# Chunk 6's ranks moved into the first batch, and eight shared chunks dealt 3, 2, 3 instead of 2, 1, 5

## The chip, the cores and the metric

One core of a Trainium2 chip runs the kernel. The metric is device time in microseconds (us) of one execution, lower is better. Before the change it is 659.68 us, the median of three runs (657.02 to 660.19).

## The reference

A state-space and convolution block with a dense MLP, then a mixture of experts, each followed by a layer norm. Batch 4 x 1024 tokens, width 128, float32. Cut to what matters:

```python
# first block
y = rmsnorm(x) * norm_w
x = x + conv3(y) + scan(tanh(a), b * y)          # along the 1024 tokens
x = x + down(silu(gate(rmsnorm(x))) * up(rmsnorm(x)))   # hidden 512
x = layernorm(x0 + x)
# second block: 64 experts of width 88 in 8 groups; 2 shared experts (176)
scores = sigmoid(x @ gate_w.T)
c = scores + gate_bias
group_scores = sum of the two largest c of each group   # keep the 4 best groups
masked = where(group kept, c, 0)
topk = the 8 largest of masked                   # experts of a token
w = 2.5 * scores[topk] / sum(scores[topk])
out = sum_k w_k * expert_k(x) + shared(x)        # expert: silu(x Wg) * (x Wu) Wd
x = layernorm(x + out)
```

## The kernel before

The 4096 tokens are 32 tiles of 128, in eight chunks of four tiles (512 tokens). Chunks 0 to 6 (28 tiles) are routed, that is, each token is sent to its eight experts. Chunk 7 is not: it goes through all 64 experts densely, with weights that are zero for experts not chosen. The routed tiles form two batches of 14 tiles.

**Front.** A loop over nine steps (`step` on TensorE, the loop over `k` on the other engines) does the first block, one chunk per step, with the routing of earlier chunks between: scores (ScalarE, `scores`), group sums and masks (VectorE, `group_sums`, `group_seconds`, `compare_groups`, `mask_groups`), the choice of eight (`choose`), and the rank of each token within its expert (`ranks`, a stream of bf16 matmuls against 0/1 tables; `take_ranks`). A rank gives the slot, a row of a DRAM buffer with a region of 2048 rows per expert. After the last chunk of a batch its table is made: `count_tiles`, `starts`, `place_tiles`, `tile_experts`, `weight_columns`. It says for each of the batch's 176 tiles of 128 slots which expert's weights and which rows belong to it.

**Scatters.** GpSimd copies every tile's tokens to their slots, eight indirect DMAs a tile, 224 in all (line 513), in order of tiles. It waits once per chunk for that chunk's slots.

**Prelude.** After the front come the two first shared chunks (`shared_block`: two blocks of two matmuls into the bank GU; a SiLU on ScalarE; `shared_hidden`, a product on VectorE; `shared_down` into the bank XT or OT; `add_shared`). Among them stand the last chunk's norm, transposition and logits, chunk 6's ranks and the second batch's table. ScalarE does root and norm of chunk 7 before the first SiLU. At the end VectorE makes all gather slots of the first batch (`gather_slots`).

**Batches.** A batch is 44 quads of four expert tiles. SyncE loads a quad's rows (line 444), from the moment that all scatters of that batch have landed. TensorE does for quad q: `tr_x` (q + 2), `gate_up` (q + 1), `tr_h` (q, line 829), `down` (q - 1). ScalarE copies x (line 1077), does the SiLU (1084), copies the output (1094) and stores it. VectorE does `mul_h` (q + 1, line 1513) and `take_h` (q, line 1522), and after it whatever stands at that quad: `slot_weights` (three operations of 512 elements; one tile at each odd quad from quad 1), the steps of chunk 7's choice (quads 2, 4, 6, 8, 10), two `gather_slots` of the second batch (12, 14), from quad 60 `add_round`. Each engine works strictly in its own written order, so an operation set between two quads holds back the next quad's. `tr_h` of the next quad needs the bank HT, hence `take_h` of this one.

One shared chunk stands between the batches, five after the second.

**Gathers and additions.** GpSimd fetches each token's eight results back by indirect DMAs (line 518), in eight sets of up to four tiles through two buffers; VectorE adds them with their weights (`add_round`, line 1576). The sets 0 to 3 belong to the first batch, 4 to 7 to the second. Ahead of the first set of a batch GpSimd waits for all stores of that batch:

```python
if ts[0] == TFIRST[b]:
    pool.wait_ge(s_gslot, 2 * b + 1)
    for r in range(4):
        pool.wait_ge(d_st[r], 4 * Q0[b + 1])
```

**Dense part.** After the last shared chunk TensorE runs 44 steps (lines 880, 881, 889) for chunk 7. Between them VectorE adds the sets 4 to 7 (`SUMS_IN_DENSE`: set: first step, rounds per step, rounds at most) and takes the statistics of the finished chunks (`STATS_IN_DENSE`, `ROOT_AT`). The last rounds, the last statistics, the norm and the last output follow.

Of the kernel before, what the change touches and what calls it, by code (L numbers as in the profile page):

```python
# [37 lines left out]
P = 128  # L38
# [9 lines left out]
E = 64  # L48
# [28 lines left out]
WT = 2  # L77
KT = 8
SH_A, SH_B = 2, 3
# [37 lines left out]
SUMS_IN_DENSE = {4: (2, 2, 8), 5: (10, 1, 8), 6: (26, 1, 8), 7: (38, 1, 5)}  # L117
STATS_IN_DENSE = {0: 0, 1: 1, 2: 2, 7: 3, 19: 4, 35: 5}
ROOT_AT = (5, 21, 37)
# [20 lines left out]
def build(nc, x, vecs, w_gate, w_up, w_down, b_down, gate_wT, gate_bias, wgu, wd, wdf, sgu, sd, out, xs, os):  # L140
    with ExitStack() as ctx:
# [25 lines left out]
        eps = sb("eps", [P, 2])  # L167
        ident = sb("ident", [P, P])
# [59 lines left out]
        score = cut(CT, E)  # L228
# [136 lines left out]
        def keys_in_psum():  # L365

            return MI[:, :].rearrange("p (t e) -> p t e", e=E)

# [109 lines left out]
        def _(pool):  # L478
# [43 lines left out]
            for g_, ts in enumerate(SETS):  # L522
# [3 lines left out]
                if ts[0] == TFIRST[b]:  # L526
                    pool.wait_ge(s_gslot, 2 * b + 1)
                    for r in range(4):
                        pool.wait_ge(d_st[r], 4 * Q0[b + 1])
# [13 lines left out]
        def _(pe):  # L543
# [102 lines left out]
            def ranks(c):  # L646
# [6 lines left out]
                mm(HT[:, 0:CT * E], ones_bf[:, :], base_bf[:, :].unsqueeze(1).to_broadcast([P, CT, E]),  # L653
                   start=True, stop=False, skip_group_check=True)
                for b in range(NBAT):
                    own = [t for t in tiles(c) if batch_of(t) == b]
                    for s in range(TFIRST[b], own[-1] if own else 0):
                        lo = max(s + 1, own[0]) - c * CT
                        n = own[-1] - c * CT + 1 - lo
                        mm(HT[:, lo * E:(lo + n) * E], ones_bf[:, :],  # L660
                           sel[:, s % (4 * CT), :].unsqueeze(1).to_broadcast([P, n, E]), start=False, stop=False,
                           skip_group_check=True)
                ins = mm(HT[:, 0:CT * E], upto_bf[:, :], flat(sel[:, ring(c), :]), start=False, stop=True,
                         skip_group_check=True)
                if c in CLAST:
                    b = CLAST.index(c)
                    for t in range(TFIRST[b], TFIRST[b + 1]):
                        ins = mm(HT[0:E, H_CNT:H_CNT + 1], sel[:, t % (4 * CT), :], ones_bf[:, 0:1],
# [3 lines left out]
            def starts(b):  # L672

                pe.wait_ge(s_nt, b + 1)
                mm(HT[:, H_START:H_START + E], ntile_bf[:, :].to_broadcast([E, P]), upto_bf[0:E, 0:E], start=True,
                   stop=True)
                mm(HT[:, H_NUM:H_NUM + E], count[:, :].to_broadcast([E, P]), ident[0:E, 0:E], start=True,
                   stop=True)
                mm(HT[0:E, H_END:H_END + 1], upto_bf[0:E, 0:E], ntile_bf[:, :], start=True,
                   stop=True).then_inc(p_start, 1)  # L680

            def tile_experts(b):

                pe.wait_ge(s_ended, b + 1)
                mm(HT[0:1, 0:ET[b]], base_col[:, 1:2], onehot[:, 0:ET[b]], start=True, stop=True)
                mm(HT[0:1, H_OFF:H_OFF + ET[b]], row_col[:, 0:1], onehot[:, 0:ET[b]], start=True,
# [68 lines left out]
            def shared_down(c):  # L755
                pe.wait_ge(s_sh, SJ * (c + 1))
                if c == 0:
                    pe.wait_ge(s_x1T, NC)
                elif c == 1:
                    pe.wait_ge(s_v, NC)  # L760
                else:
# [5 lines left out]
                dst = OT if c % 2 else XT  # L767
# [6 lines left out]
            def shared_from(lo, hi):  # L774
                for c in range(lo, hi):
                    shared_block(c, 0)
                    shared_block(c, 1)
                    if c == 0:
                        transpose_x1(NS, NC + 1)
                    if c == 1:  # L780
                        ranks(NS - 1)
                    if c > lo:
                        shared_down(c - 1)
                    if c == 1:
# [979 lines left out]
```

## Time and profile before

| | |
|---|---|
| median of three runs | 659.68 us |
| profiled execution | 659.67 us |
| its span | 657.9 us |
| TensorE matmul (PE), busy | 588.1 us, 89% |
| VectorE (DVE) | 461.0 us, 70% |
| GpSimd (POOL) | 444.8 us, 68% |
| ScalarE (ACT) | 325.7 us, 50% |

The span is the stretch from the first to the last instruction that the profile holds. PEld is TensorE's weight load, which overlaps PE. PEclk is the clock granted to TensorE as a share of full speed (1.0 is 2.4 GHz, 0.5 is 1.2 GHz). In a timeline the first two numbers are start and duration in us, then engine, line of the kernel, operation, output and inputs, how many were merged, and in brackets how long the engine had been idle and what released it ("issue" is nothing that the profile shows). In groups of instructions the columns are line, engine, operation, output and inputs, count, then busy us and mean ns of one, then the idle time ahead of them and what ended most of it.

### The profile page before, as it was taken

How to read it: one execution, taken by the hardware profiler on the slowest of the kernel's cores; microseconds unless marked ns; L12 is line 12 of the kernel's file. 1: busy time of each engine (PE TensorE's matmuls, PEld its weight loads, DVE VectorE, ACT ScalarE, POOL GpSimd, SP SyncE). 2: the span in 40 equal slices, each digit the busy share in tenths (PEclk: the TensorE clock that was granted, in tenths of full speed). 3: DMA queues.
4: the chain of work that ended last, by engine and by line, in shares of the span. 5: the costliest groups of instructions: out<-in, count | busy, mean ns of one | idle time of the engine just before them, and what ended most of it. 6: DMA issues, size and time to landing. Idle time of an engine off the chain costs nothing.

```text
span 657.9 us, 13016 instructions
## 1 busy us (share of the span) xinstructions
PE 588.1 (89%) x3456; PEld 472.5 (72%) x3457; DVE 461.0 (70%) x1311; ACT 325.7 (50%) x637; POOL 444.8 (68%) x464
## 2 busy tenths in 40 slices
PE   2986988888889899999996999999999999999980
PEld 2655666665655899999994999999995666666640
DVE  3446688888756789767773567677475598868785
ACT  8474866665553454555552455555552135252332
POOL 1003777777777777777776777777764777777773
PEclk9988899998997999999998999999999999999995
DMA  8962666661112678777755688888866223222122
GB/s 211 383 133 52 138 156 144 148 141 53 53 49 84 179 230 237 230 227 224 230 159 141 184 235 228 242 232 234 228 198 203 53 53 95 56 69 65 52 65 64
DMA packets 124609, 101.35 MB, mean 154 GB/s; under 512 B 15334, under 2 KB 114494, under 8 KB 124094
## 3 DMA queue, kind: packets, MB, share of 16 engines
q1 hardware_dynamic: 63766, 48.41, 27.9%
q0 software_dynamic: 14336, 29.39, 15.3%
q10 hardware_dynamic: 46464, 23.07, 12.1%
q8 instruction: 16, 0.26, 0.2%
q14 instruction: 27, 0.22, 0.1%
HBM read 52.58 MB, written 48.23 MB: 153 GB/s over the span
## 4 chain that ended last, share of the span: by engine, by line
PE 41%; POOL 31%; issue 12%; DVE 5%; DMA 4%; ACT 3%; SPq 1%; POOLq 0%; DVEq 0%; ACTq 0%
POOL xs_dram L513 29%; PE GU L820 8%; PE OT L840 6%; PE GU L880 4%; PE GU L881 4%; PE XT L889 4%; PE HT L829 3%; PE XT L809 3%; DMA arena<-os_dram,gslots 2%; POOL arena L518 2%; PE GU L601 1%; PE GU L752 1%; PE GU L751 1%; DMA xs_dram<-x1r,slots 1%; SPq L444 1%
## 5 line engine op out<-in xcount | busy, mean ns | idle before, releaser
L513 POOL DMA_INDIRECT xs_dram<-x1r,slots x224 | 225.7, 1007 | 123.5 <-issue 67.5
L518 POOL DMA_INDIRECT arena<-os_dram,gslots x224 | 217.0, 969 | 80.6 <-issue 64.8
L820 PE MATMUL GU<-wgu_sb,arena 128*128 x704 | 121.5, 316 | 0.1
L820 PEld LDWEIGHTS GU<-wgu_sb,arena 128*128 128x128 f32 x704 | 106.3, 192 | 1.2 <-issue 0.9
L1513 DVE TENSOR_TENSOR mlpw_sb<-GU,mlpw_sb 128x352 f32<-128x352 f32 x88 | 46.1, 524 | 73.6 <-ACT mlpw_sb L1084 70.0
L840 PE MATMUL OT<-wd_sb,arena 88*128 x704 | 93.7, 276 | 1.8 <-ACT ol L1094 1.7
L1094 ACT ACTIVATE ol<-OT 128x512 f32<-128x512 f32 x88 | 52.5, 597 | 80.7 <-PE OT L840 80.7
L840 PEld LDWEIGHTS OT<-wd_sb,arena 88*128 88x128 f32 x704 | 85.5, 192 | 3.0 <-issue 2.6
L1576 DVE SCALAR_TENSOR_TENSOR x_all<-arena,wk,x_all 128x128 f32<-128x128 f32 x224 | 66.3, 344 | 4.7 <-DMA arena<-os_dram,gslots 2.8
L1084 ACT ACTIVATE mlpw_sb<-GU 128x352 f32<-128x352 f32 x88 | 40.7, 463 | 49.3 <-PE GU L820 48.7
L1188 ACT ACTIVATE key<-GU 128x512 f32<-128x512 f32 x44 | 26.2, 596 | 69.9 <-PE GU L881 69.8
L1522 DVE COPY arena<-HT 88x512 f32<-88x512 f32 x88 | 59.6, 677 | 0.8 <-PE HT L829 0.8
L809 PE MATMUL XT<-ident,arena 128*128 128x128 f32 x352 | 54.4, 277 | 4.7 <-DMA arena<-xs_dram 3.0
L1077 ACT ACTIVATE arena<-XT 128x512 f32<-128x512 f32 x88 | 52.2, 593 | 12.4 <-PE XT L809 10.2
L829 PE MATMUL HT<-ident,mlpw_sb 128*88 128x128 f32 x352 | 52.8, 273 | 1.6 <-DVE arena L1522 1.6
L880 PE MATMUL GU<-x_all,wgu_sb 128*128 128x512 f32 x88 | 45.8, 602 | 1.5 <-DVE x1r L1487 0.9
L809 PEld LDWEIGHTS XT<-ident,arena 128*128 128x128 f32 x352 | 41.8, 143 | 6.9 <-DMA arena<-xs_dram 4.9
L881 PE MATMUL GU<-x_all,wgu_sb 128*128 128x512 f32 x88 | 44.9, 592 | 0.0
L829 PEld LDWEIGHTS HT<-ident,mlpw_sb 128*88 128x88 f32 x352 | 40.6, 122 | 4.2 <-DVE mlpw_sb L1513 1.3
L601 PE MATMUL GU<-arena,mlpw_sb 128*128 128x512 f32 x64 | 37.5, 671 | 6.8 <-DVE arena L1262 6.0
L1614 DVE TENSOR_TENSOR key<-GU,key 128x512 f32<-128x512 f32 x44 | 30.1, 685 | 18.6 <-PE XT L889 10.3
L880 PEld LDWEIGHTS GU<-x_all,wgu_sb 128*128 128x128 f32 x88 | 28.1, 327 | 17.4 <-issue 8.7
(206 smaller groups left out, 897.2 us busy)
## 6 DMA issues: line engine op xcount, KB each, us to landing
arena<-xs_dram SPq DMA_DIRECT2D x352, 64.0 KB
os_dram<-ol ACTq DMA_DIRECT2D x88, 256.0 KB
xs_dram<-ol SPq DMA_DIRECT2D x16, 512.0 KB
wgu_sb<-wgu_dram SPq DMA_DIRECT2D x1, 5632.0 KB
xs_dram<-x1r,slots POOLq DMA_INDIRECT x224
arena<-os_dram,gslots POOLq DMA_INDIRECT x224, 2.6
wd_sb<-wd_dram SPq DMA_DIRECT2D x1, 2816.0 KB
x_all<-x_dram SPq DMA_DIRECT2D x8, 256.0 KB, 5.7
```

The source lines that it names most:

```text
L513: g.indirect_dma_start(out=xs[b], out_offset=bass.IndirectOffsetOnAxis(ap=slots[:, t * K + k:t * K + k + 1], axis=0), in_=x1r[:, t, :], in ...
L518: return g.indirect_dma_start(out=gbuf[:, g_ % 2, t - SETS[g_][0], k, :], out_offset=None, in_=os[batch_of(t)], in_offset=bass.IndirectOff ...
L809: ins = tr(XT[:, i * P:(i + 1) * P], xl[:, u % 4, i * P:(i + 1) * P], ident[:, :])
L820: ins = mm(GU[:, 2 * r + i // 2, (i % 2) * 2 * I:(i % 2 + 1) * 2 * I], xg[:, r, i * P:(i + 1) * P], wgu_sb[:, bass.ds(at[i], 2 * I)], star ...
L829: ins = tr(HT[0:I, i * P:(i + 1) * P], eh[:, u % 2, i * I:(i + 1) * I], ident[:, :])
L840: ins = mm(OT[:, i * P:(i + 1) * P], hT[0:I, u % 2, i * P:(i + 1) * P], wd_sb[:, bass.ds(at[i], P)], start=True, stop=True)
L880: mm(GU[:, r, :], wgu_sb[:, j:E * 2 * I:I], x1T(NS), start=True, stop=True)
L881: mm(GU[:, r + 1, :], wgu_sb[:, HI + j:E * 2 * I:I], x1T(NS), start=True, stop=True).then_inc(p_dg, 1)
L1077: f(xg[:, u % 2, :], XT[:, :], ACT.Copy).then_inc(s_xg, 1)
L1094: f(ol[:, u % 4, :], OT[:, :], ACT.Copy).then_inc(s_eo, 1)
L1522: v.tensor_copy(hT[0:I, u % 2, :], HT[0:I, :]).then_inc(s_ht, 1)
L1576: v.scalar_tensor_tensor(out=x_all[:, t, :], in0=gbuf[:, g % 2, t - SETS[g][0], kk, :], scalar=wk[:, t * K + kk:t * K + kk + 1], in1=x_all ...
```

## The change

`SH_A` and `SH_B` go from 2, 3 to 3, 5: three shared chunks ahead of the first batch, two between the batches, three after the second. In the prelude the SiLUs of chunks 0 and 1 come ahead of the root and norm of chunk 7; chunk 2's down goes to the bank HT. Chunk 6's `ranks` follow quad 1 of the first batch on TensorE, `starts` quad 3, `tile_experts` quad 5, now in the bank MI; VectorE has the steps that belong to them, and the first batch's gather slots in two halves, among quads 1 to 6. Chunk 7's choice moves to quads 5, 7, 8, 10 and 13, slot weights start at quad 9 and end at quad 63. Slot and dense normalisation of the second batch go to quads 68 and 70. The steps of the dense part at which sets are added move back by one to five. In every choice `scores` writes `rw` itself, the mask is a comparison and a predicated copy of zeros, and the multiplication by the 0/1 table is left out except for chunk 7. The cut diff:

```diff
+W0 = 9
-SH_A, SH_B = 2, 3
+SH_A, SH_B = 3, 5
-SUMS_IN_DENSE = {4: (2, 2, 8), 5: (10, 1, 8), 6: (26, 1, 8), 7: (38, 1, 5)}
+SUMS_IN_DENSE = {4: (3, 2, 8), 5: (15, 1, 8), 6: (30, 1, 8), 7: (40, 1, 2)}
+        def rank_bank(c):
+            return MI if c == NS - 1 else HT
+        def shared_bank(c):
+            return HT if c == 2 else OT if c % 2 else XT
...
# TensorE
-            shared_from(0, SH_A)      # with ranks(6), logits(7), starts(1), tile_experts(1) in it
+            for c in range(SH_A):
+                shared_block(c, 0)
+                shared_block(c, 1)
+                if c:
+                    shared_down(c - 1)
+            pe.wait_ge(s_res, 1)
+            transpose_x1(NS, NC + 1)
+            shared_down(SH_A - 1)
+            logits(NS)
...
+                n = UN if b else 2 * UN
+                for u in range(n):
+                    quad(b, Q0[b] + u, u % UN)
+                    if b == 0 and u == 1:
+                        ranks(NS - 1)
+                    if b == 0 and u == 3:
+                        starts(NBAT - 1)
+                    if b == 0 and u == 5:
+                        tile_experts(NBAT - 1)
...
# ScalarE
-            root_v(NS)
-            norm_v(NS)
             for c in range(SH_A):
                 for j in range(SJ):
                     shared_silu(c, j)
+                if c == SH_A - 2:
+                    nc.scalar.preload_act_table(ACT.Sqrt)
+                    root_v(NS)
+                    nc.scalar.preload_act_table(ACT.Silu)
+                    norm_v(NS)
...
# VectorE, mask_groups and choose
-                then(v.tensor_scalar(m2, m1, GONE, None, ALU.is_equal))
-                then(v.tensor_tensor(ch4, ch4, bc(m2.unsqueeze(2), P, n, EG), ALU.mult))
-                then(v.tensor_scalar(choice, choice, 0.0, None, ALU.add))
+                then(v.tensor_scalar(m2, m1, GONE, None, ALU.not_equal))
+                then(v.copy_predicated(ch4, bc(m2.bitcast(U32).unsqueeze(2), P, n, EG),
+                                       bc(zero[:, 0:1].unsqueeze(2), P, n, EG)))
-                v.tensor_tensor(rw[:, span(c), :], sel[:, ring(c), :], score, ALU.mult).then_inc(s_sel, 1)
+                else:
+                    v.tensor_scalar(sel[:, ring(c), :], tab_a, GONE, None, ALU.is_equal).then_inc(s_sel, 1)
...
# VectorE, first batch
+            for q in range(Q0[1]):
                 quad(0, q, q)
+                if q == 1:
+                    gather_slots(0, 0, half0)
                 if q == 2:
+                    take_ranks(NS - 1)
+                    count_tiles(NBAT - 1)
+                if q == 3:
+                    gather_slots(0, half0, TFIRST[1])
+                if q == 4:
+                    place_tiles(NBAT - 1)
+                if q == 5:
                     group_sums(NS)
+                if q == 6:
+                    weight_columns(NBAT - 1)
+                if q == 7:
                     group_seconds()
+                if q == 8:
                     compare_groups()
+                if q == 10:
                     mask_groups()
+                if q == 12:
+                    gather_slots(1, TFIRST[1], half1)
+                if q == 13:
                     choose(NS)
+                if q == 14:
+                    gather_slots(1, half1, NST)
                 if q == Q0[1] - 2 * UN:
                     normalize_slots(0, TFIRST[1])
+                if q % 2 and q >= W0:
+                    slot_weights((q - W0) // 2)
...
# VectorE, adding in the second batch
+                    q = SUM_AT[g] + k
                     quad(b, q, q)
+                    if q % 2 and q < 2 * NST + W0:
+                        slot_weights((q - W0) // 2)
+                    if q == SUM_AT[1]:
+                        normalize_slots(TFIRST[1], NST)
+                    if q == SUM_AT[1] + 2:
+                        normalize_dense()
                     add_round(g, k)
...
-                    for k in range(3 * (c - SH_B - 1), min(K, 3 * (c - SH_B))):
+                    for k in range(4 * (c - SH_B - 1), min(K, 4 * (c - SH_B))):
                         add_round(3, k)
```

## Rows read from the trace of the kernel before

**Rows 1.** Groups by line, GpSimd, 505.2 to 650 us; columns as on the page.

```profile
L518 POOL DMA_INDIRECT arena<-os_dram,gslots x112 | 109.6, 979 | 40.1 <-issue 34.9 <-DMA arena<-os_dram,gslots 2.7 <-DVE x_all L1576 2.4
```

**Rows 2.** Timeline, GpSimd (start, us, engine, line, operation, count, idle before).

```profile
505.25 0.94 POOL L518 DMA_INDIRECT arena<-os_dram,gslots  x1 [5.19 <-issue]
...
648.80 0.94 POOL L518 DMA_INDIRECT arena<-os_dram,gslots  x1 [0.30 <-issue]
```

**Rows 3.** Timeline, SyncE's queue, end of the second batch.

```profile
504.25 0.33 SPq L466 DMA_DIRECT2D ol<-wdf_dram  x1
```

**Rows 4.** Timeline, TensorE, shared downs and last dense matmul.

```profile
508.47 1.95 PE L771 MATMUL XT<-sd_sb,key 88*128 88x128 f32 x16
...
513.69 1.95 PE L771 MATMUL OT<-sd_sb,mlpw_sb 88*128 88x128 f32 x16
...
640.18 1.12 PE L889 MATMUL XT<-key,ol 128*128 128x512 f32 x2 [1.64 <-DVE key L1616]
```

**Rows 5.** Timeline, GpSimd's scatters, the 33rd and the last.

```profile
100.56 0.96 POOL L513 DMA_INDIRECT xs_dram<-x1r,slots  x1 [0.75 <-issue]
...
351.21 0.96 POOL L513 DMA_INDIRECT xs_dram<-x1r,slots  x1 [0.30 <-issue]
```

**Rows 6.** Timeline, TensorE, first batch: quads 1 and 4, transpose of quad 2.

```profile
214.41 0.63 PE L809 MATMUL XT<-ident,arena 128*128 128x128 f32 x4 [0.78 <-ACT arena L1077]
...
223.36 0.66 PE L809 MATMUL XT<-ident,arena 128*128 128x128 f32 x4 [1.03 <-DMA arena<-xs_dram]
...
225.13 0.60 PE L829 MATMUL HT<-ident,mlpw_sb 128*88 128x128 f32 x4
```

**Rows 7.** Timeline, TensorE, third shared chunk and second batch's quads 44, 46, 47.

```profile
350.93 1.02 PE L751 MATMUL GU<-x_all,sgu_sb 128*88 128x512 f32 x2
...
359.06 1.12 PE L809 MATMUL XT<-ident,arena 128*128 128x128 f32 x4 [0.78 <-DVE x_all L1487]
...
371.94 0.60 PE L829 MATMUL HT<-ident,mlpw_sb 128*88 128x128 f32 x4
...
374.91 0.60 PE L829 MATMUL HT<-ident,mlpw_sb 128*88 128x128 f32 x4
```

**Rows 8.** Windows, prelude: PE, PEld, DVE, ACT, POOL busy, PEclk, DMA, GB/s.

```profile
194.00:198.60 4.60, 0.67 (x5) 0.47 (x5) 0.98 (x3) 4.40 (x8) 3.38 (x5) 0.84 0.14 43
198.60:204.00 5.40, 5.40 (x7) 1.90 (x8) 4.28 (x19) 0.68 (x2) 4.18 (x5) 0.50 0.21 65
```

**Rows 9.** Windows, columns as rows 8: ranks, starts, tile experts.

```profile
204.70:206.82 2.12, 2.12 (x30) 1.83 (x28) 0.69 (x1) 1.88 (x2) 1.72 (x2) 1.00 0.20 62
209.62:210.24 0.62, 0.62 (x6) 0.51 (x5) 0.00 (x0) 0.47 (x2) 0.38 (x1) 1.00 0.41 112
212.10:212.92 0.82, 0.78 (x5) 0.24 (x4) 0.69 (x2) 0.00 (x0) 0.54 (x1) 1.00 0.64 182
```

**Rows 10.** The page's groups: copy of the transposed h.

```profile
L1522 DVE COPY arena<-HT 88x512 f32<-88x512 f32 x88 | 59.6, 677 | 0.8 <-PE HT L829 0.8
```

**Rows 11.** Timeline, VectorE's multiplications and TensorE's transposes, quads 10 to 13.

```profile
250.45 0.52 DVE L1513 TENSOR_TENSOR mlpw_sb<-GU,mlpw_sb 128x352 f32<-128x352 f32 x1
...
253.91 0.52 DVE L1513 TENSOR_TENSOR mlpw_sb<-GU,mlpw_sb 128x352 f32<-128x352 f32 x1
...
257.09 0.52 DVE L1513 TENSOR_TENSOR mlpw_sb<-GU,mlpw_sb 128x352 f32<-128x352 f32 x1
...
255.40 0.60 PE L829 MATMUL HT<-ident,mlpw_sb 128*88 128x128 f32 x4
...
258.61 0.60 PE L829 MATMUL HT<-ident,mlpw_sb 128*88 128x128 f32 x4
```

**Rows 12.** Windows, columns as rows 8: start of the second batch.

```profile
359.00:365.50 6.50, 5.50 (x25) 5.04 (x26) 0.44 (x2) 2.12 (x4) 4.97 (x6) 0.59 0.60 162
```

**Rows 13.** Timeline, VectorE, one round of four additions.

```profile
415.55 1.13 DVE L1576 SCALAR_TENSOR_TENSOR x_all<-arena,wk,x_all 128x128 f32<-128x128 f32 x4
```

**Rows 14.** Windows, VectorE alone: the dense normalisation.

```profile
409.60:411.60 2.00, 1.86 (x7) 1.00 0.70 191
```

More of the change, by code:

```diff
@@ L858, in first_quads @@
                 gate_up(Q0[b], 0)
-                for u in range(UN):
-                    quad(b, Q0[b] + u, u)
-                with pe.Fori(Q0[b] // UN + 1, Q0[b + 1] // UN - 1) as i:
+                n = UN if b else 2 * UN
[7 more added lines that the diff above has]
+                        tile_experts(NBAT - 1)
+                with pe.Fori((Q0[b] + n) // UN, Q0[b + 1] // UN - 1) as i:
                     for u in range(UN):
@@ L1139, in last_quads @@
                     quad(b, Q0[b + 1] - UN + u, u)
+                    if b == 0 and (Q0[1] - UN + u) % (2 * KT) == W0 - 1:
+                        copy_keys(Q0[1] // (2 * KT))
                 take_out(Q0[b + 1] - 1, UN - 1)
@@ L1315, in group_sums @@
                 dve.wait_ge(s_sc, c + 1)
-                then(v.tensor_tensor(choice, score, bc(gbias_sb[:, :].unsqueeze(1), P, CT, E), ALU.add))
+                then(v.tensor_tensor(choice, rw[:, span(c), :], bc(gbias_sb[:, :].unsqueeze(1), P, CT, E), ALU.add))
                 lo, hi = ch4[:, :, 0:EG // 2], ch4[:, :, EG // 2:EG]
@@ L1623, in plain @@
                             quad(b, i * UN + u, u)
-            def weighed(b, lo, hi):
-                for q in range(lo, hi):
-                    quad(b, q, q)
-                    if q % 2:
-                        slot_weights(q // 2)
             def adding(b, g):
                 for k in range(K):
-                    quad(b, SUM_AT[g] + k, SUM_AT[g] + k)
+                    q = SUM_AT[g] + k
+                    quad(b, q, q)
+                    if q % 2 and q < 2 * NST + W0:
+                        slot_weights((q - W0) // 2)
@@ L1671, in _ @@
             mul_h(Q0[1], 0)
-            weighed(1, Q0[1], 2 * NST)
-            for q in range(2 * NST, 2 * NST + UN):
+            for q in range(Q0[1], SUM_AT[0]):
                 quad(1, q, q)
-                if q == 2 * NST:
-                    normalize_slots(TFIRST[1], NST)
-                if q == 2 * NST + 2:
-                    normalize_dense()
+                if q % 2:
+                    slot_weights((q - W0) // 2)
             adding(1, 0)
```

118 lines of the change are left out of this document (48 added, 70 removed).

## The prediction

> **What bounds the kernel now.** I read the groups of the stretch after the second batch first, then GpSimd's timeline there, then the starts of the two batches. The chain of waits that the page prints is misleading at the end: it runs through TensorE's dense matmuls up to 612 us and only then changes to GpSimd's gathers. But from 505.25 us to 648.80 us GpSimd issues the second batch's 112 gathers without a real pause [rows 1, 2]: of 40.1 us idle, 34.9 are its own issue time, about 0.3 us each, and only 5.1 us are waits for a DMA or for VectorE. These gathers may start when all stores of the second batch have landed; SyncE, which waits for the same stores, goes on at 504.25 us [rows 3]. TensorE, beside them, does five shared chunks at 5.22 us each (two downs stand 513.69 - 508.47 apart) and 44 dense steps, and its last dense matmul starts at 640.18 us, over 8 us before the last gather [rows 4]. So the end is tied like this: scatters end (351.21 + 0.96 us, [rows 5]), second batch on TensorE, its stores, 112 gathers, output. The reader is to see that TensorE's work after the second batch is not on that path, and that a us at the end of the second batch is a us at the end of the kernel.
>
> In the first batch TensorE waits for loads up to 223.36 us (1.03 us there) and is then its own bound: the transposes of h follow each other at 2.97 us [rows 6, 7]. The execution took 659.67 us (span 657.9 and 1.8 outside it); the median of the runs is 659.68, so a shift of the span is a shift of either.
>
> **The change part by part.**
>
> *Front: fewer VectorE operations for a choice.* The rank matmuls no longer wait for a 0.43 us multiplication, and a mask is two operations for three. The scatter chain was once gated by VectorE: at 100.56 us GpSimd had been idle 0.75 instead of 0.30 us [rows 5]. I take that 0.45 us as gained by all that follows. Bounds: nothing, and 1.2 us if the first scatter starts earlier too. The predicated copy does not occur before; its nearest rows are the operations that it replaces, so between half and twice their 0.7 us, far below what would matter at one place per chunk.
>
> *Prelude: a third shared chunk, SiLUs first, ranks out.* Before, TensorE worked 0.67 us in 194.0 to 198.6, because the SiLU waited behind the last chunk's root and table load; then 5.40 us at a granted clock of 0.50, and it was done at 213 [rows 8]. Out go the ranks, starts and tile experts (3.52 us, [rows 9]), in comes one chunk (5.22), and the 3.9 us hole is filled: 213 - 3.5 + 5.2 - 3.9 = 210.8 us. The loads decide the first batch (its fifth quad waited for one until 223.36, [rows 6]), so this chunk costs nothing and the earlier end gains nothing. If the hole stayed, the prelude would end at 214.7, and most of the 1.7 us would go into the 1.03 us wait.
>
> *First batch: TensorE gets the ranks.* They now stand in a stream that is TensorE-bound. Ranks 2.12 us after quad 1, less the 1.03 us wait for a load at that place: +1.1. Starts 0.62 after quad 3, tile experts 0.78 after quad 5 [rows 9]: together +2.5, of which I let 0.3 vanish in small pauses of that stretch: +2.2 us. Their own waits are covered: VectorE reaches the counts and the table some 1 to 2 us before TensorE asks. Bounds: 0.8 (all pauses absorbed) and 3.5 (one wait open).
>
> *First batch: VectorE.* It does a multiplication (0.52) and a copy (0.68, [rows 10]) per quad, about 1.1 us from start to start since they overlap. The quad with the choice took 3.46 us, the one with slot weights 3.18 [rows 11]. Together these two ran 0.71 us over twice 2.97, on 0.2 us of lateness brought along, and the next transpose came at 3.21 instead of 2.97 [rows 11]: 0.24 us of stall, so about 0.7 us of lateness is free. In the change quad 13 holds the choice of the last chunk and slot weights: 3.46 + 3.18 - 1.1 = 5.54, 2.57 over the pitch, 1.9 us of stall, for the 0.24 of before: +1.65 us. The other extras of quads 1 to 8 (half tables, ranks, counts, group sums) are each at most about as long as one slot-weight quad, whose work left these quads, so nothing there. Bounds 0 (slack elsewhere) and 2.6.
>
> *Between the batches: two chunks for one.* One chunk went from 350.93 to the second batch's first transpose at 359.06, 8.13 us, of which 5.22 are work [rows 4, 7]. Two chunks cover each other's SiLU waits and leave about 1 us for the last addition: 350.93 + 10.44 + 1.0 = 362.4, 3.3 us later. After that the loads have landed and nothing waits for DMA. In the first batch the third transpose of h (225.13) came 10.7 us after the second transpose of x (214.41), 9.7 without the load wait [rows 6]; the second transpose of x will stand about 1.4 us after 362.4 (an estimate: four transposes, 0.66, and the 0.6 us copy that frees their bank), so the third transpose of h is at 373.5 instead of 371.94 [rows 7]: +1.6 us. Bounds 0.3 and 3.5 (nothing covered).
>
> Here the clock counts. From 359.0 to 365.5 us the granted clock was 0.59, mostly the lower level (1.2 GHz), after TensorE had paused in the chunk [rows 12]. The Trainium skill ("TensorE: Matmul & The Clock Gate", What's actually happening) says that idling is what puts the clock down and sustained work what brings it back; the trace agrees (0.50 also after the hole of [rows 8]). With two chunks back to back I take the full clock; by the row, were it low again, 0.41 of 5.50 us, 2.3 us more.
>
> *Second batch: VectorE.* Slot weights shift by eight quads, so two of them fall into quads 61 and 63, which also add a round of four (1.13 us, [rows 13]): 3.18 + 1.13 = 4.3, 1.35 over the pitch, 0.65 of stall each. The dense normalisation (1.86 us busy, [rows 14]) falls into quad 70 beside a round: 1.1 + 1.95 + 1.15 = 4.2, 0.5 us of stall. Slot normalisation with a round stays within the slack. +1.8 us; bounds 0 and 2.5.
>
> *Tail: three chunks for five.* TensorE and VectorE save 2 x 5.22 = 10.4 us, and the additions in the dense loop are put about four steps later to match. This is cost 0 and gain 0, since GpSimd's 112 gathers hide it; its cover would have to shrink by over 8 us before it counted. Bounds: 2 us less if fewer gathers meet busy VectorE, 1 more.
>
> Sum: -0.45 + 2.2 + 1.65 + 1.6 + 1.8 = +6.8 us, so 659.67 + 6.8 = **666.5 us**, slower by 1.0%. The bounds add to -2.1 and +13.1; not all fall on one side.
>
> **The rivals.**
>
> (a) *The tail counts: faster.* If TensorE's tail set the end, the 10.4 us would be gained: 666.5 - 10.4 = 656.1 us. For it: the chain of waits follows the dense matmuls, and the last additions wait for both. Against: the gathers have no gap that a faster TensorE could close [rows 1], and the last dense matmul is early [rows 4]. It decides from the point where GpSimd waits for additions; there are 2.4 us of such waits in 145. Chance 0.12. The Trainium skill ("Perfetto Trace Analysis", Optimization Strategies) says that the goal is in general to keep the matmul engine busy; by that rule alone this rival is right, since the change fills TensorE's hole in the prelude.
>
> (b) *The extras fit.* The additions to VectorE's quads are absorbed, and only ranks and the middle cost: -0.45 + 1.1 + 1.6 = 2.3, 662 us, no measurable change. For it: VectorE is busy only a good two thirds of the time. Against: the 0.24 us stall that a lighter pair of quads already showed [rows 11]. Chance 0.18.
>
> (c) *The prelude is too long.* It stays at the lower clock, as it was for 5.40 us, with a chunk more: some 6 us later than 210.8, past the loads, and the first batch starts about 3 us late: 669.5 us. For it: the 0.50 in [rows 8]. Against: the hole in front of it goes. Chance 0.08.
>
> **How the numbers follow.** The forecast (664 to 668.5 by itself) has the remaining 0.62. This kernel can tell about 0.5%, 3.3 us, from no change: faster means below 656.4, slower above 663.0. Faster: most of (a), 0.11 in all. Same: (b), the rest of (a) and a little of the forecast's low end, 0.19. Slower: 0.70. The range of 660 to 670 us leaves out (a) and the case in which most upper bounds meet.
>
> **What would show it.** First batch: the ranks' matmuls between the second and third transposes of h, the load wait at the fifth quad gone, one pitch of about 4.9 us after quad 13. Middle: two chunks, the second batch's first transpose at about 366, clock 1.0. Second batch: pitches over 3.3 us near quads 61, 63 and 70. Tail: the dense loop ends about 3 us before where it did, while the first gather after the stores starts near 512 and the last near 655. I am wrong if the first gather starts at or before 506, or if the gathers take clearly less than 143 us.

## The result: 1.7% slower, and where the trace after puts it

The changed kernel took 670.17 us (median, 668.47 to 671.28) beside 658.82 us for the kernel before on the same chip, a ratio of 1.0172 [1.0136, 1.0207]. The direction was forecast; the time lies 3.7 us above the forecast of 666.5 and just outside the range to 670. Measured once more beside other kernels it took 667.87 us (665.49 to 673.08), ratio 1.0115 [1.0085, 1.0144], which lies inside the range. The direction is clear both times, the size is not. Its ten executions lie in two groups, three at 665.5 to 665.9 us with a mean clock of 0.959 to 0.961, seven at 668.5 to 673.1 with 0.950 to 0.957. The profiled execution took 670.12 us, 10.45 more than the one of before. All the arithmetic below is between these two profiles.

The first view is TensorE's timeline in the first batch (start, us, engine, line, operation, count, idle before; line 841 is the transpose of h, one a quad). It answers to [rows 6, 11].

```profile
217.23 0.60 PE L841 MATMUL HT<-ident,mlpw_sb 128*88 128x128 f32 x4
219.30 0.60 PE L841 MATMUL HT<-ident,mlpw_sb 128*88 128x128 f32 x4
224.47 0.60 PE L841 MATMUL HT<-ident,mlpw_sb 128*88 128x128 f32 x4
...
261.53 0.60 PE L841 MATMUL HT<-ident,mlpw_sb 128*88 128x128 f32 x4
266.18 0.61 PE L841 MATMUL HT<-ident,mlpw_sb 128*88 128x128 f32 x4 [1.52 <-DVE arena L1544]
268.97 2.30 PE L832 MATMUL GU<-wgu_sb,arena 128*128 x8
271.10 0.60 PE L841 MATMUL HT<-ident,mlpw_sb 128*88 128x128 f32 x4
```

A pitch is the time from one transpose of h to the next. The ranks make the pitch up to the third transpose 5.17 us, and after quad 13 two pitches are 4.65 and 4.92 for the usual 2.97. The first of these is VectorE's: TensorE waits 1.52 us for its copy. The second is mostly something else: the gate and up matmuls at 268.97 take 2.30 us instead of 1.36, at a granted clock of 0.50 to 0.59 from 268.0 to 271.3 us.

The second view is the same engine between the batches. It answers to [rows 7].

```profile
350.39 0.61 PE L841 MATMUL HT<-ident,mlpw_sb 128*88 128x128 f32 x4 [1.14 <-DVE arena L1544]
350.93 1.15 PE L852 MATMUL OT<-wd_sb,arena 88*128 x8
352.95 2.07 PE L852 MATMUL OT<-wd_sb,arena 88*128 x8 [0.87 <-ACT ol L1112]
354.82 1.92 PE L762 MATMUL GU<-x_all,sgu_sb 128*88 128x512 f32 x2
...
360.64 1.02 PE L762 MATMUL GU<-x_all,sgu_sb 128*88 128x512 f32 x2
...
364.08 1.95 PE L784 MATMUL OT<-sd_sb,mlpw_sb 88*128 88x128 f32 x16
...
368.60 0.66 PE L821 MATMUL XT<-ident,arena 128*128 128x128 f32 x4 [0.79 <-DVE x_all L1511]
...
370.91 2.52 PE L832 MATMUL GU<-wgu_sb,arena 128*128 x8
...
374.90 0.60 PE L841 MATMUL HT<-ident,mlpw_sb 128*88 128x128 f32 x4
...
379.99 0.60 PE L841 MATMUL HT<-ident,mlpw_sb 128*88 128x128 f32 x4
```

From the first batch's last transpose of h (350.39) to the second batch's third (379.99) it is 29.60 us; before it was 371.94 - 347.42 = 24.52, with the same two pauses at its head:

```profile
347.42 0.61 PE L829 MATMUL HT<-ident,mlpw_sb 128*88 128x128 f32 x4 [1.14 <-DVE arena L1522]
...
349.94 1.15 PE L840 MATMUL OT<-wd_sb,arena 88*128 x8 [0.87 <-ACT ol L1094]
```

In the changed kernel the first chunk takes 5.82 us (354.82 to 360.64), the second 3.44 (360.64 to 364.08). The windows of this stretch (length, PE busy, granted clock, DMA share, GB/s) show why:

```profile
352.90:359.80 6.90, 6.85 (x15) 0.51 0.65 188
359.80:369.80 10.00, 8.67 (x47) 1.00 0.22 59
369.80:373.80 4.00, 3.77 (x17) 0.57 0.59 154
```

TensorE paused 1.14 and 0.87 us at the end of the batch, and the clock fell to its lower level (1.2 GHz) before the chunks began, not behind them as in [rows 12]. It rose, and fell again after the pauses of about 0.8 us around 368 to 370.

The last view is the end of the second batch: the last transpose of h before and after, then, of the changed kernel, ScalarE's queue with the last stores, SyncE's queue, GpSimd's gathers, and their group. It answers to [rows 1 to 3].

```profile
492.87 0.61 PE L829 MATMUL HT<-ident,mlpw_sb 128*88 128x128 f32 x4 [0.47 <-DVE arena L1522]
...
502.19 0.61 PE L841 MATMUL HT<-ident,mlpw_sb 128*88 128x128 f32 x4 [0.66 <-DVE arena L1544]
```

```profile
505.92 1.45 ACTq L1117 DMA_DIRECT2D os_dram<-ol  x2
505.95 0.34 SPq L472 DMA_DIRECT2D arena<-wdf_dram  x1
514.94 0.33 SPq L475 DMA_DIRECT2D ol<-wdf_dram  x1
515.94 0.94 POOL L527 DMA_INDIRECT arena<-os_dram,gslots  x1 [9.06 <-DVE x_all L1598]
...
659.27 0.94 POOL L527 DMA_INDIRECT arena<-os_dram,gslots  x1 [0.30 <-issue]
...
L527 POOL DMA_INDIRECT arena<-os_dram,gslots x112 | 109.4, 977 | 43.9 <-issue 28.1 <-DVE x_all L1598 11.8 <-DMA arena<-os_dram,gslots 4.0
```

The releaser that the trace names for the gather at 515.94, an addition, is not it: SyncE waits for the same stores and goes on at 514.94. The 112 gathers then take 143.33 us (143.55 before).

| step | forecast, us | by the two traces, us |
|---|---|---|
| start of the first batch | -0.45 | -1.47 (217.23 for 218.70) |
| ranks, starts, tile experts | +2.2 | +1.68 |
| VectorE at quad 13 | +1.65 | +1.43, and 1.33 by the clock |
| between the batches | +1.6 | +5.08 |
| second batch, VectorE | +1.8 | +1.27 |
| stores of the second batch | 0 | +1.37 |
| last gathers and the end | 0 | -0.24 |

The right column adds to the 10.45 us measured. The second row is 3.67 us of longer pitches less 1.99 that stood there before (1.39 by the load wait, 0.60 four quads on).

### The profile page after: what moved, and what is told of

Read it like the earlier page. It is cut to its first block, busy times and chain, and to the rows that moved or that the text cites. A ratio compares the mean times of both kernels' runs of the same rounds, so it can differ in the third digit from the quotient of the medians.

```text
span 668.4 us, 12969 instructions
## 1 busy us (share of the span) xinstructions
PE 588.9 (88%) x3456; PEld 475.9 (71%) x3457; DVE 457.4 (68%) x1299; ACT 325.7 (49%) x637; POOL 444.3 (66%) x464
## 4 chain that ended last, share of the span: by engine, by line
PE 65%; POOL 15%; issue 7%; DVE 5%; ACT 4%; DMA 3%; SPq 0%; POOLq 0%; DVEq 0%; ACTq 0%
PE GU L832 16%; POOL xs_dram L522 12%; PE OT L852 12%; PE XT L821 6%; PE HT L841 6%; PE GU L899 5%; PE GU L900 5%; PE XT L908 5%; POOL arena L527 3%; DMA arena<-os_dram,gslots 2%; PE GU L762 2%; PE GU L763 1%; PE OT L631 1%; PE GU L610 1%; PE GU L611 1%
## 5 line engine op out<-in xcount | busy, mean ns | idle before, releaser
L832 PE MATMUL GU<-wgu_sb,arena 128*128 x704 | 123.2, 319 | 0.0
L832 PEld LDWEIGHTS GU<-wgu_sb,arena 128*128 128x128 f32 x704 | 108.9, 196 | 0.2 <-issue 0.2
L610 PE MATMUL GU<-arena,mlpw_sb 128*128 128x512 f32 x64 | 36.1, 647 | 7.9 <-DVE arena L1283 5.9
```

What stands on the lines that cost most here:

```text
L832: ins = mm(GU[:, 2 * r + i // 2, (i % 2) * 2 * I:(i % 2 + 1) * 2 * I], xg[:, r, i * P:(i + 1) * P], wgu_sb[:, bass.ds(at[i], 2 * I)], star ...
```

## Experiments

My theory: the path is TensorE through both batches, then the stores, then 112 gathers, and what exceeds the forecast is TensorE's clock, on the step between the batches above all. Rivals: the tail counts after all; or the delays are absorbed by the first batch's gathers. Each ratio is to the kernel before on the same chip. "Middle" is the stretch of 29.60 us above, measured alike in each.

**The changed kernel again**, as the baseline.

> The changed kernel itself once more, unaltered, as the baseline beside the three others. Both theories: 668 to 671 us. Clock theory: of the spread between its executions a large part is TensorE's clock, so a profile with fewer low stretches is shorter by their worth; store and load times at the batch ends differ by up to 1.4 us from one execution to the next.

667.87 us, 1.0115 [1.0085, 1.0144]. The profiled execution was the longest, 673.08, with a middle of 29.56 and the same two falls of the clock; its stores landed 1.15 us later still (14.90 us from the last transpose of h to the first gather; 13.75 in the first profile, 12.38 before). So the store term varies by more than a us from one execution to the next.

The middle varies too. Four of the kernels below leave it as it is, and in their profiles it is 27.97 us (the choice after quad 12), 26.57 (the ranks ahead), 26.61 (the additions later) and 26.59 (the dense weights later). In the first two the clock fell only ahead of the chunks, in the last two only ahead of the second batch; none was without a fall. TensorE in the profile with the later additions:

```profile
350.32 0.61 PE L841 MATMUL HT<-ident,mlpw_sb 128*88 128x128 f32 x4 [1.14 <-DVE arena L1544]
...
352.89 1.15 PE L852 MATMUL OT<-wd_sb,arena 88*128 x8 [0.87 <-ACT ol L1112]
353.88 1.02 PE L762 MATMUL GU<-x_all,sgu_sb 128*88 128x512 f32 x2
...
367.25 2.40 PE L832 MATMUL GU<-wgu_sb,arena 128*128 x8
```

The pauses of 1.14 and 0.87 us are those of the changed kernel, yet the down and the chunks behind them run at the full clock (1.02 us a pair of matmuls for 1.92). So a profile below can hold up to 3 us that its edit did not cause, and what an edit does is read from its own stretch of the trace.

**One chunk between the batches.** `SH_A, SH_B = 3, 4`

> The changed kernel with one shared chunk between the batches instead of two (three ahead, one, four after). Path theory: the second batch moves forward by one chunk's matmuls, 3.4 us, if TensorE's clock falls before the chunk as it did at 352.9 us in the changed kernel, and by up to 6.5 us (3.4 for the chunk and 3.1 for the clock) if it stays at 1.00 there; the fourth chunk of the tail stays hidden behind the gathers. So 664 to 667 us. Rival, the tail counts: the chunk only changes its place, and 670 us stay, or 1.8 us more (5.2 us less 3.4). Third transpose of h of the second batch 24.5 to 26.2 us after the first batch's last one, where the changed kernel has 29.6.

665.79 us, 1.0083 [1.0059, 1.0107]; the middle is 26.17 us, 3.43 less than in the changed kernel's own profiles, where the second chunk took 3.44. The clock fell at both places as there, so the lower branch of the expectation holds. The chunk in the tail cost nothing: the last 112 gathers took 142.81 us.

**No chunk between.** `SH_A, SH_B = 3, 3`

> The changed kernel with no shared chunk between the batches (three ahead, none, five after, the tail of the kernel before). Path theory: the second batch's first transpose of x no longer waits for two chunks (354.8 to 368.5 us in the changed kernel), the second batch ends some 13 us earlier, before GpSimd has issued the first batch's 112 gathers; these then are the limit, 359.7 + 112 x 1.28 = 503 us, and the last 112 follow for 143.3 us: first gather after the stores at 501 to 504 instead of 515.9, the end 12 to 15 us earlier, 655 to 658 us. Rival, the tail counts: of 13 us at most 2.6 are left when two chunks more (10.4 us) stand in the tail: 667 us or more. Rival, the loads decide: without chunks TensorE waits for loads, and 5 us at most are gained: 665 us.

666.13 us, 1.0092 [1.0060, 1.0124]: 8 to 11 us above the 655 to 658 expected. TensorE did its part, the last transpose of h of the second batch stands at 491.71 instead of 502.19. GpSimd's timeline shows what took over:

```profile
360.87 0.98 POOL L527 DMA_INDIRECT arena<-os_dram,gslots  x1 [11.31 <-DMA os_dram<-ol]
...
495.97 0.94 POOL L527 DMA_INDIRECT arena<-os_dram,gslots  x1 [4.61 <-DMA arena<-os_dram,gslots]
...
504.26 0.94 POOL L527 DMA_INDIRECT arena<-os_dram,gslots  x1 [3.60 <-DMA arena<-os_dram,gslots]
...
511.87 0.98 POOL L527 DMA_INDIRECT arena<-os_dram,gslots  x1 [0.30 <-issue]
```

The last 112 gathers (from 511.87) no longer wait for stores but follow the first batch's directly, and those started late and waited 8.2 us for landings. The path now runs from the first batch's stores through all 224 gathers, and a faster second batch is worth nothing there. The tail as such is refuted as a limit: with 10.4 us more of TensorE's work in it, the last 112 gathers take 143.41 us as ever.

**Added work in TensorE's pauses**, which tests the clock alone.

```diff
+def idle_work(bank, n):
+    for i in range(n):
+        tr(bank[:, 0:P], ident[:, :], ident[:, :])
 # ahead of the first batch's last tr_h: idle_work(XT, 8)
 # ahead of its last down:               idle_work(XT, 7)
 # ahead of the second batch's tr_x:     idle_work(HT, 7)
```

> The changed kernel with added work that nothing reads: 8 transposes of the identity before the first batch's last transpose of h, 7 before its last down matmuls and 7 before the second batch's first transpose of x, where TensorE otherwise pauses for about 1 us each. Clock theory: the clock stays at 1.00 through the end of the first batch and the two chunks, 3.1 us gained, and up to 4.7 if the second batch's first gate and up matmuls (2.52 us at the low clock, 1.36 at the full one) run at full speed too: 665.5 to 667 us. Rival: the clock falls anyway, or what is gained before the second batch is waited away at its first loads: 670 us.

665.09 us, 1.0086 [1.0064, 1.0108]. The windows of the same stretch, and the two transposes of h that bound the middle:

```profile
352.90:359.80 6.90, 6.90 (x23) 1.00 0.66 191
359.80:369.80 10.00, 9.21 (x69) 1.00 0.33 90
369.80:373.80 4.00, 4.00 (x35) 1.00 0.59 164
```

```profile
350.16 0.61 PE L841 MATMUL HT<-ident,mlpw_sb 128*88 128x128 f32 x4 [0.26 <-DVE arena L1553]
...
375.10 0.60 PE L841 MATMUL HT<-ident,mlpw_sb 128*88 128x128 f32 x4
```

The clock stays at 1.00 and the middle is 24.94 us: 4.66 less than in the changed kernel's first profile, the upper figure of the expectation, and 1.6 to 3.0 less than in the four others with the same stretch. More work made the same chunks shorter, so the pauses and the clock are the cause. The device time does not show the size, since the later additions came to 665.34 us beside it without this work. The Trainium skill ("TensorE: Matmul & The Clock Gate", What's actually happening) says that the monitor which sets the clock runs freely, so that the count of slow matmuls at a kernel's start differs between runs of the same kernel; the trace agrees for pauses within a kernel, with the middle at 26.57 to 29.60 us for the same instructions, but no run here shows the monitor's phase.

**The choice after quad 12**, where no slot weights stand.

```diff
 if q == 12:
-    gather_slots(1, TFIRST[1], half1)
-if q == 13:
     choose(NS)
 if q == 14:
+    gather_slots(1, TFIRST[1], half1)
+if q == 16:
     gather_slots(1, half1, NST)
```

> The changed kernel with the choice of the last chunk after quad 12, where no slot weights stand, instead of quad 13; the two halves of the second table move from quads 12 and 14 to 14 and 16. Path theory: the stall after quad 13 (pitches of 4.65 and 4.92 us for 2.97) goes, by 1.65 us as predicted and up to 3.0 us by the changed kernel's trace (of its 3.6 us some 0.6 stood before the change too): 667 to 668.5 us. Rival, the stall is absorbed by VectorE's slack later in the batch or by GpSimd: 670 us, no difference. The middle has two chunks as before, so it also shows whether TensorE's clock falls again at the end of the first batch (last down matmuls 2.07 us for 1.15).

664.83 us, 1.0068 [1.0045, 1.0092], where 667 to 668.5 was expected; the middle was 1.63 us shorter in the profile besides. From first to last transpose of h the batch takes 130.26 us for 133.16:

```profile
262.90 0.60 PE L841 MATMUL HT<-ident,mlpw_sb 128*88 128x128 f32 x4
266.08 0.60 PE L841 MATMUL HT<-ident,mlpw_sb 128*88 128x128 f32 x4
269.51 0.60 PE L841 MATMUL HT<-ident,mlpw_sb 128*88 128x128 f32 x4
```

The pitches are 3.18 and 3.43: 2.9 us came from VectorE's queue at one quad, some 1.6 of it stall and 1.3 the clock that fell behind the stall (priced below).

**The ranks ahead of the first transpose of x.** `ranks(NS - 1)` moves from quad 1 to the head of `first_quads(0)`.

> The changed kernel with the ranks of chunk 6 (2.1 us on TensorE) ahead of the first batch's first transpose of x, where TensorE waited 2.98 us for the first load and its clock fell to 0.50, instead of after the second quad. Path theory: 2.1 us leave the stream that is TensorE's own, the first transpose of x comes up to 1.2 us later (the choice ends near 208.7, so the ranks at about 211 where the transpose stood at 209.9): 1 us gained, and up to 2.5 more if the clock stays up (the first quads ran at 0.50 until about 215.6): 667 to 669 us. Rival, the loads decide the start: the later start eats the gain, 670 us. Fifth pitch pattern: the 5.17 us pitch of the third transpose of h goes back to about 3.

669.18 us (661.41 to 671.93), 1.0120 [1.0089, 1.0151], no gain: the rival. The 5.17 us pitch is 3.08, 2.1 us less as expected, but the first transpose of h stands at 219.63 us (216.7 to 218.7 in the others), and the clock stayed low until 219 (from 209). Work moved into a wait for a load was waited away.

**Additions that meet no slot weights.** `SUM_AT = {0: 64, 1: 72, 2: 80}`

> The changed kernel with the first additions of gathered rows at quads 64 and 72 instead of 60 and 68, so that no round of four meets slot weights (the last ones follow quad 63). Path theory: the pitches of 3.24 and 4.03 us in the second batch become 2.97, 1.3 us earlier from there to the end: 669 us where the unaltered one has 670. Rival, that stretch is absorbed because GpSimd's gathers of the first batch end only 9 us before the stores and now wait for later additions: no difference, or up to 2 us slower.

665.34 us, 1.0088 [1.0067, 1.0109]. The pitches in question are 2.97, and from third to last transpose of h the second batch takes 120.87 for 122.20 us: 1.33 less, as forecast. The time fell by 2.5 us and not by 1; in the profile the middle was 3 us shorter too, by the clock alone. In this execution the stall after quad 13 was there (1.52 us) but the clock did not fall, and the next gate and up matmuls took 1.46 us, not 2.30:

```profile
267.45 0.61 PE L841 MATMUL HT<-ident,mlpw_sb 128*88 128x128 f32 x4 [1.52 <-DVE arena L1544]
...
269.75 1.46 PE L832 MATMUL GU<-wgu_sb,arena 128*128 x8
271.04 0.60 PE L841 MATMUL HT<-ident,mlpw_sb 128*88 128x128 f32 x4
```

The pitch is 3.59 us for the 4.92 of the changed kernel with the same instructions: 1.33 us is the price of this one fall. Of nine profiles with the choice after quad 13, five show the fall and four do not.

**Transfers put back**, in the kernel without a chunk between.

```diff
 for b in range(NBAT):
+    if b:
+        for r in range(4):
+            sp.wait_ge(d_st[r], 4 * Q0[b])
     sp.wait_ge(s_woff, b + 1)
...
+for r in range(4):
+    sp.wait_ge(d_st[r], 4 * NQ)
 sp.wait_ge(p_tx, NQ)
 sp.dma_start(wdf_mid[:, 0:half], ...)
...
-for r in range(4):
-    sp.wait_ge(d_st[r], 4 * NQ)
 sp.dma_start(flat(ol[:, :, :])..., ...)
```

> The kernel without a chunk between the batches, and with SyncE's transfers put back: the second batch's loads wait until the first batch's stores have landed, and the dense weights wait for the second batch's stores. There the first gathers stood 9.25 us behind the first batch's last transpose of h (7.77 in the kernel before, whose loads came later), and the gathers waited 4.61 and 3.60 us for landings while the dense weights were loaded. Theory of contention: the first gather comes 1.5 us sooner and the two waits go, 1.5 + 8.2 us earlier at the end: 656 to 658 us. Rival: the gathers' landings are slow by themselves and the loads' delay of some 3 us costs TensorE: 666 to 668 us.

663.48 us, 1.0044 [1.0021, 1.0067], 2.7 us less and not 8 to 10. Both waits went and the first gather came 7.50 us behind the transpose, as contention has it; but the later loads make the middle 24.36 us (18.03 without them), and the end of the second batch is the limit again:

```profile
358.03 0.97 POOL L530 DMA_INDIRECT arena<-os_dram,gslots  x1 [8.31 <-DMA os_dram<-ol]
...
504.77 0.94 POOL L530 DMA_INDIRECT arena<-os_dram,gslots  x1 [4.39 <-issue]
```

**Only the dense weights later**, in the changed kernel and in the kernel before (the second and third part of that diff).

> The changed kernel with one edit: SyncE loads the dense weights only when the second batch's stores have landed, not from the last transposes of x on. Theory of contention: the first gather after these stores stands 7.9 us behind the batch's last transpose of h, as in the kernel where the transfers were put back, instead of 13.8 to 14.9 us; of that some 5 us arrive at the end, less up to 2 us because the weights then meet the first of the last gathers: 663 to 665 us where the unaltered kernel has 667.9. Rival: the stores land late by themselves: 668 us. Rival: the weights come too late for the dense steps: 668 us or more.

> The kernel before with the same edit. Theory of contention: first gather after the stores 7.9 instead of 12.4 us behind the last transpose of h, 3 to 4.5 us faster: 655 to 657 us, unless the first batch's gathers (their last at 499.12 us) then become the limit, which leaves 505.25 - 500.4 = 4.9 us at most. Rival: no difference, 659.7 us.

664.80 us, 1.0092 [1.0058, 1.0126], and 657.83 us, 0.9973 [0.9959, 0.9988]. In the changed kernel (SyncE's queue, then gathers):

```profile
505.12 0.34 SPq L471 DMA_DIRECT2D arena<-wdf_dram  x1
...
506.05 0.95 POOL L527 DMA_INDIRECT arena<-os_dram,gslots  x1 [5.19 <-issue]
...
514.18 0.94 POOL L527 DMA_INDIRECT arena<-os_dram,gslots  x1 [2.44 <-DMA arena<-os_dram,gslots]
```

From the last transpose of h to the first gather it is 8.64 us for 13.75, in the kernel before 8.32 for 12.38. The weights then meet the gathers, which wait 2.44 (3.60 in the kernel before) and take 144.83 us (146.37) in all. By the ratios 1.5 to 1.8 us arrive; in the changed kernel, whose executions run from 661.73 to 670.26, that is within the interval, in the kernel before it is clear of it. The kernel before with this edit is the quickest of all that ran, and quicker than both kernels of this study.

**All corrections without a chunk between, with the ranks early too, and with free loads.** The first has the choice after quad 12, additions at 64 and 72, transfers put back, added work (8, 7, 40); the second adds the early ranks; the third lets the second batch's loads start at once and has added work only at the first batch's end.

> The kernel without a chunk between the batches with four edits together: transfers put back (loads behind the first batch's stores, dense weights behind the second's), choice after quad 12, additions at 64 and 72, and added transposes of the identity that nothing reads in TensorE's pauses at the end of the first batch (8 and 7) and ahead of the second (40). Path theory, from the single runs: last transpose of h of the first batch at 347.6, first gather 7.5 us later at 355.1, 112 gathers in 142.6 us: 497.8; second batch: 24.4 us to its third transpose of h, 2 less with the clock up, then 120.9: 490.9 to 492.9, stores 7.9: 499 to 501. The larger holds: last 112 gathers from 499 to 501 (before: 505.3), 654 to 657 us, faster than the kernel before by 0.4 to 0.9%. Rival: the edits do not add, since each moved another limit: 660 to 663 us.

> The same with a fifth edit: the ranks of chunk 6 ahead of the first transpose of x. By its single run the ranks cost 2.1 us less in the stream (7.25 to 5.15 us from the first to the third transpose of h) and the first transpose of h came 1.1 us later: 1 us earlier than the version with four edits, 653 to 656 us. Rival: the longer low clock at the start (208 to 218 us in that run) takes it back: no difference, or 1 us slower.

> The version without chunks between the batches with the choice after quad 12, additions at 64 and 72, dense weights behind the stores and the transposes at the first batch's end (8 and 7), but with the second batch's loads free to start beside the first batch's stores. By the single runs: last transpose of h at 348.8, stores landed 9.3 us later (7.5 to 7.9 where the loads wait), 112 gathers in 142.6 us: 500.7; the second batch is done before, 348.8 + 18.0 + 120.8 + 8.7 = 496.3. So the last gathers start at 501 to 502 instead of 503.1 where the loads wait: 657.5 to 659 us. Rival, the gathers of the first batch meet more traffic and wait 4 us or more, as they did without a chunk: 661 us or more.

659.57 us, 0.9989 [0.9975, 1.0003]; 660.26, 1.0012 [0.9994, 1.0031]; 659.35, 0.9996 [0.9978, 1.0014]. None beats the kernel before, where 653 to 659 us were expected, and the early ranks gained nothing here either. The first has the last 112 gathers from 503.10, 2 to 4 us later than I worked out: the clock fell during the longer wait for the loads (to 0.50, from about 361 to 367), so the middle was 24.71. In the third the second batch is done at 488.88, the middle being 19.05, and again the first batch's gathers decide, with a wait of 4.47 us for a landing ahead of the last 112 at 505.42, as the rival said.

**All corrections, the split kept.** Two chunks between the batches, as in the change; choice after quad 12, additions at 64 and 72, late weights, added work (8, 7, 7).

> The changed kernel with its two chunks between the batches and four edits that leave the split alone: choice after quad 12, additions at 64 and 72, dense weights behind the stores, and the added transposes (8, 7, 7). If stall, clock and transfers are all that the change costs beyond its ranks, the last transpose of h of the first batch stands at 348, the second batch's third 24.9 us later, then 120.8 and 8.6 to the last gathers at 502.3: 657.5 to 660 us, as the version without chunks between (659.6). Rival, two chunks cost by themselves in that place: 662 us or more.

659.22 us, 1.0002 [0.9982, 1.0021]: the changed order with stall, clock and transfers corrected is as quick as the kernel before. The middle is 24.94 us, as with the added work alone. It took 0.9 us more than the kernel before with the same late weights and added work (658.29, next), so the order itself is no gain.

**The added work in the kernel before**, alone and with late weights.

> The kernel before with the same added transposes of the identity that nothing reads (8 and 7 at the end of the first batch, 7 before the second). If the clock costs the kernel before as it costs the changed one, its third transpose of h of the second batch comes 22 to 23 us behind the first batch's last one instead of 24.5, and the time is 657 to 658 us. Rival, there TensorE waits for the second batch's loads, which start when the scatters are done, and the clock costs nothing net: 659.5 us; then the clock is a price of the changed order alone.

> The kernel before with two edits: dense weights behind the second batch's stores, and the added transposes. If both gains add, 655.5 to 657 us (657.8 with the first edit alone); the first batch's gathers (last at 496.04 us there, the next possible at 497.3) allow 2.4 us more than the 499.7 of that run. Rival, the loads hide the clock: 657.8 us.

659.67 us, 1.0001 [0.9985, 1.0017], and 658.29, 0.9974 [0.9958, 0.9990]. The first's middle is 23.22 us, 1.30 less than 24.52, at a clock of 1.00: the clock does cost the kernel before, 1.3 us in its profile. It did not reach the end, because the first batch's gathers waited:

```profile
494.55 1.04 POOL L518 DMA_INDIRECT arena<-os_dram,gslots  x1 [3.89 <-DVE x_all L1585]
...
503.46 0.94 POOL L518 DMA_INDIRECT arena<-os_dram,gslots  x1 [4.12 <-DMA arena<-os_dram,gslots]
...
505.96 0.95 POOL L518 DMA_INDIRECT arena<-os_dram,gslots  x1 [0.30 <-issue]
```

In the second the gains do not add: its ratio is that of the late weights alone (0.9973). There the added work did not hold the clock. TensorE waited 1.26 and 1.96 us for the second batch's loads, the clock was 0.63 from 366 to 370 us, and the middle was 25.94.

## Why the prediction was right in direction and short by 3.7 us

*What bounds the kernel* was right. With the dense weights loaded where both kernels have them, the last 112 gathers took 142.8 to 144.9 us with three, four and five chunks in the tail, so rival (a) falls, and in the changed kernel every delay up to the second batch's end arrived.

*The step that failed* is "between the batches": "With two chunks back to back I take the full clock." At the full clock the two chunks were sized well: with the added work it is 11.43 us from their start to the second batch's first transpose of x, for 11.44 forecast. The whole stretch was then 24.94 us, 0.42 over the 24.52 of the kernel before for the 1.6 forecast, because from the second transpose of x to the third of h it took 8.52 us for the 9.7 that I had taken from the first batch. But the clock fell ahead of the chunks, in the pauses at the end of the first batch, which the two chunks do nothing about, and once more ahead of the second batch. That cost 4.66 us in the changed kernel's profile, and 0.42 + 4.66 makes the 5.08 measured. In the four other profiles of the same stretch it cost 1.6 to 3.0, so the full clock was wrong in every one, and the size of the miss was in part luck: the profile that I compare had both falls, and that the second measurement, 667.87, came to lie in the range is luck of the same kind. The 24.52 holds a price of the clock too, 1.30, where the low stretch lay beside waits for loads. I had put the price of a low clock at 2.3 us, from one place, and left it out of the sum.

*First batch.* Ranks +1.68 for +2.2: the load wait hid more. VectorE's doubled quad: 1.43 for 1.65; that the clock falls behind the stall, in some executions, was not thought of, and cost 1.33 more. Rival (b), the extras fit, falls with the choice after quad 12: 2.9 us.

*Second batch.* +1.27 for +1.8; taking the collisions away gave 1.33 back. The pitches up to the transposes of quads 63 and 64 were 0.27 and 1.06 us over the usual one, and near quad 70 only one was, by 0.1 for the 0.5 forecast.

*Stores* were put at nothing. With the dense weights loaded beside them the first gather stands 12.3 to 14.9 us behind the last transpose where the stores decide it, without 7.9 to 9.1. Of the 1.37 us between the two profiles none is shown to be the change's own. SyncE, which waits for the stores, goes on 11.31 to 13.90 us behind that transpose in the changed kernel and its variants with these loads, and 11.38 and 11.99 us in two profiles of the kernel before.

*Front and prelude.* The prelude is done before the loads, and TensorE waits 2.98 us for the first of them. Its first transpose of x stands at 209.86 us, 3.12 earlier than before (212.98), so the earlier end did gain something there, against the forecast. But after that wait the clock was 0.50 up to 216 us, where it had been 1.00, and 1.47 us reached the first transpose of h. That start at 217.23 is no proof of more: the kernels with the same front start between 216.7 and 218.7, the kernel before and its variants between 217.9 and 220.8. The idle of 0.75 us at the 33rd scatter is 0.30 in the changed kernel, so the 0.45 us of the front are there, but these starts vary too much to show that they arrive. Rival (c), a prelude past the loads, did not occur.

Open: why the clock fell in some executions after the pauses of 1.14 and 0.87 us and held in others. It held in the profile of the kernel before and in two of six profiles of the changed kernel's two chunks without added work. No profile without added work was free of a fall, and a shorter end of the batch was not tried.

## What to carry to other kernels

Before costing a step that stands behind a drain of the pipeline, read the granted clock from the drain on and price the step at both levels; a pause of 1 us may be paid again as slower matmuls after it. Read the same stretch in several executions before crediting an edit with what the clock did. When a change shortens one of two chains that meet in a wait, work out the other chain's time first: here 10.5 us less on TensorE brought the last gather 4 us forward, as the gathers' chain was next. Ask which transfers run beside the last stores of a stage, since who waits for these stores waits for the others too.

## What I had not expected of the hardware

With the same instructions around it, the clock fell after a pause of 1.52 us in some profiles (gate and up matmuls 2.30 us) and not in others (1.46). 22 transposes that nobody reads, about 3 us of work put into pauses, made the stretch around them 1.6 to 4.7 us shorter, by what the clock had done there without them. Loading the dense weights beside the last stores delayed their landing by 4 to 5 us.
